# A language-model tower on one core: the first normalisation's statistics as running sums on ScalarE

## The reference

```python
h = weight[ids] * keep_mask[ids]                  # (32, 512, 256)
n = (h - mean(h)) / sqrt(var(h) + 1e-5)           # first normalisation, over the 256
u, res = split(n @ in_proj_w.T, [512])            # 512 and 256 wide
u = causal_conv(u, conv_w, taps=4) + conv_b       # along the tokens, channel by channel
g = u * sigmoid(softplus(u @ dt_proj_w.T + dt_proj_b))
y = scan(state = 0.9 * state + 0.1 * g)           # along the tokens
h = h + y @ out_proj_w.T + res                    # h2 in the kernel
n2 = (h - mean(h)) / sqrt(var(h) + 1e-5)          # second normalisation
h = h + quantised(n2) @ quantised(ffn_w).T + ffn_b
```

## Time and profile before

| | |
|---|---|
| median of 3 runs | 1020.15 us (1020.0 to 1021.33) |
| the profiled execution | 1021.15 us |
| its span, first to last instruction | 1019.3 us |
| PE busy | 956.8 us (94%) |
| DVE busy | 946.7 us (93%) |
| ACT busy | 577.6 us (57%) |
| POOL busy | 721.3 us (71%) |
| mean granted PE clock | 0.991 of full speed |

### The profile page before, as it was taken

How to read it: one execution, slowest core, us unless ns; L and a number is a source line. 1 busy time by engine, 2 the same in 40 slices (tenths; PEclk the granted TensorE clock), 3 DMA queues, 4 the chain that set the end, 5 groups by cost and what they waited for, 6 DMA issues and landing times.

```text
span 1019.3 us, 14858 instructions
## 1 busy us (share of the span) xinstructions
PE 956.8 (94%) x4892; PEld 788.0 (77%) x4892; DVE 946.7 (93%) x1594; ACT 577.6 (57%) x966; POOL 721.3 (71%) x586
## 2 busy tenths in 40 slices
PE   3599999999999999999999999999999999999996
PEld 2377888788788888878887878878887888787885
DVE  4779999999999999999999999999999999999866
ACT  4455655655565665565565556566556556555441
POOL 5656777877677877677788767787767777876561
PEclk9899999999999999999999999999999999999998
DMA  4223323334323434333334432343433343442201
GB/s 150 62 63 95 90 86 105 116 112 125 95 81 92 124 103 124 107 86 95 103 105 122 123 93 78 97 124 103 124 103 86 96 106 103 124 124 84 77 28 41
DMA packets 73787, 100.78 MB, mean 99 GB/s; under 512 B 12576, under 2 KB 61088, under 8 KB 73760
## 3 DMA queue, kind: packets, MB, share of 16 engines
q1 hardware_dynamic: 67616, 83.59, 26.7%
q0 software_dynamic: 6144, 16.85, 7.5%
HBM read 51.65 MB, written 48.76 MB: 99 GB/s over the span
## 4 chain that ended last, share of the span: by engine, by line
PE 48%; POOL 26%; issue 14%; DVE 8%; ACT 4%; DMA 1%; POOLq 0%; DVEq 0%
POOL g_lo L370 7%; PE psZ L1033 6%; POOL u_lo L377 6%; POOL rows L355 6%; PE psZ L1026 6%; PE psZ L1027 5%; POOL h L402 3%; PE psT L984 3%; PE psU L969 3%; PE psT L980 3%; PE psU L965 3%; PE psT L981 3%; PE psU L966 3%; ACT n L541 2%; PE psO L1070 2%
## 5 line engine op out<-in xcount | busy, mean ns | idle before, releaser
L370 POOL TENSOR_TENSOR g_lo<-g,g_hi 128x512 fp32r<-128x512 f32 x128 | 201.6, 1586 | 210.4 <-ACT g_hi L499 210.4
L707 DVE SCALAR_TENSOR_TENSOR u<-psU,cw,u 128x511 f32<-128x511 f32 x378 | 258.2, 739 | 4.2 <-ACT u L481 1.5
L1026 PE MATMUL psZ<-u_hi,dt_hi 128*128 128x512 f32 x512 | 204.0, 399 | 12.8 <-ACT u_hi L488 6.8
L1033 PE MATMUL psZ<-u_lo,dt_hi 128*128 128x512 f32 x512 | 206.6, 404 | 6.7 <-POOL u_lo L377 5.6
L1027 PE MATMUL psZ<-u_hi,dt_lo 128*128 128x512 f32 x512 | 203.2, 397 | 0.0
L377 POOL TENSOR_TENSOR u_lo<-u,u_hi 128x512 fp32r<-128x512 f32 x128 | 163.0, 1296 | 11.4 <-ACT u_hi L488 10.6
L499 ACT ACTIVATE g_hi<-g 128x512 fp32r<-128x512 f32 x128 | 77.0, 625 | 132.0 <-DVE g L791 131.9
L355 POOL DMA_INDIRECT rows<-table,ids x128 | 126.1, 985 | 30.9 <-issue 29.6
L488 ACT ACTIVATE u_hi<-u 128x512 fp32r<-128x512 f32 x128 | 80.5, 629 | 109.9 <-DVE u L707 106.0
L1033 PEld LDWEIGHTS psZ<-u_lo,dt_hi 128*128 128x128 f32 x512 | 96.6, 189 | 44.5 <-POOL u_lo L377 21.9
L1026 PEld LDWEIGHTS psZ<-u_hi,dt_hi 128*128 128x128 f32 x512 | 96.8, 189 | 32.3 <-issue 7.2
(11 more groups left out here) (110 smaller groups left out, 2181.7 us busy)
## 6 DMA issues: line engine op xcount, KB each, us to landing
turned_n<-nb_blocks SPq DMA_DIRECT2D x31, 512.0 KB
nT<-turned_n SPq DMA_DIRECT2D x124, 128.0 KB
out<-h SPq DMA_DIRECT2D x31, 512.0 KB, 2.9
turned<-xb SPq DMA_DIRECT2D x30, 512.0 KB, 2.6
xT<-turned SPq DMA_DIRECT2D x120, 128.0 KB
rows<-table,ids POOLq DMA_INDIRECT x128
dt_stage<-dt_wT SPq DMA_DIRECT2D x1, 1024.0 KB, 5.7
g<-in_wT SPq DMA_DIRECT2D x1, 768.0 KB, 4.7
```

Of the source, the lines that this page charges most:

```text
L370: pool.tensor_tensor(g_lo[:, m, :], g[:, m, :], f32(g_hi[:, m, :]), ALU.subtract).then_inc(g_lo_ready[m], 1)
L707: dve.scalar_tensor_tensor(u[:, m, back:T], u_psum_tile(st, m)[:, 0:T - back], cw[:, m, TAPS - 1 - back:TAPS - back], u[:, m, back:T], ALU ...
L1026: pe.matmul(psZ[:, m % 2, :], dt_hi[:, k, o], u_hi[:, k, :], start=(k == 0), stop=False)
L1033: ins = pe.matmul(psZ[:, m % 2, :], dt_hi[:, k, o], u_lo[:, k, :], start=False, stop=(k == M - 1))
```

## The change

The mean and the variance of the first normalisation no longer come from `bn_stats` and `bn_aggr`, apart from those of sequence 0. `mask_rows` gives out the sum of each masked row as it writes it (`accum_out`). GpSimd makes `-mean` and `-mean / 16` of it. ScalarE then takes the square of `(h - mean) / 16`, and the running sum of those 256 squares is the variance; GpSimd adds the epsilon. The squares themselves are written to `n1` and are not used.

The first normalisation is made for sequence `s + 2` at the end of `u`'s part of step `s`, instead of for `s + 1` at its beginning, and `turn_n1` and its transfers go with it. `split_nT` still works on sequence `s + 1`, whose transfers are then those of the step before; it stands one place earlier on VectorE and one place later on ScalarE. `nm2` and `ve2` of the second normalisation are made by GpSimd at the head of `inverse_root2`. The four gathers of a step fetch sequence `s + 3` and stand behind `inverse_root2`; `add_bias` goes to the head of GpSimd's step. Six small constant tiles are set at the start in place of two.

```diff
-        ids = sb("ids", [P, 2, C], I32)
+        ids = sb("ids", [P, RING, C], I32)
...
@@ SyncE @@
-                if st.front:
-                    sp.wait_ge(nT_lo_ready, s + 1)
-                    sp.wait_ge(n_turned, s + 1)
+                for ahead in st.turn_ahead:          # (1, 2) in step 0, then (2,)
+                    sp.wait_ge(n_turned, s + ahead)
+                    sp.wait_ge(nT_lo_ready, s + ahead)
...
@@ GpSimd @@
+                def mean1(ahead):
+                    pool.wait_ge(h_ready, s + ahead + 1)
+                    pool.tensor_tensor(nm1[:], sum1[:], minus_mean[:], ALU.mult)
+                    pool.tensor_tensor(nm1_part[:], sum1[:], minus_mean_part[:],
+                                       ALU.mult).then_inc(mean1_ready, 1)
+
+                def variance1(ahead):
+                    pool.wait_ge(square1_ready, s + ahead)
+                    pool.tensor_tensor(ve1[:], square1[:], eps[:], ALU.add).then_inc(var1_ready, 1)
...
                 def inverse_root2(part):
-                    pool.wait_ge(var2_ready, s + (part or 0))
+                    pool.wait_ge(aggr2_done, count)
...
+                    pool.tensor_tensor(nm2[:, cs], mv2[:, cs, 0], minus_1[:, cs], ALU.mult).then_inc(mean2_ready, 1)
+                    pool.tensor_tensor(ve2[:, cs], mv2[:, cs, 1], eps[:, cs], ALU.add).then_inc(var2_ready, 1)
...
-                if st.front:
-                    inverse_root1()
+                if st.tail:
+                    add_bias()
                 if st.back:
                     split_g(M - 1, s - 1)
-                if st.gather:
-                    gather(st.b, st.ring(2)[0], (0, 1))
-                if st.main:
-                    split_u(0)
-                    split_u(1)
-                if st.gather:
-                    gather(st.b, st.ring(2)[0], (2, 3))
-                if st.tail:
-                    add_bias()
+                if st.first:
+                    variance1(1)
+                    inverse_root1(1)
+                if st.early:
+                    mean1(2)
+                split_u(0)
+                split_u(1)
+                if st.early:
+                    variance1(2)
+                    inverse_root1(2)
...                                                # split_u(2), (3), split_xT
                 if st.back:
                     inverse_root2(None)
+                if st.gather:
+                    gather_ahead()                 # the four gathers of s + 3
...                                                # split_g(0) to (2)
@@ ScalarE @@
                         ins = act.activation(h[:, ring, c, :], h[:, ring, c, :], ACT.Copy,
-                                             scale=rows[:, ring, c, D:D + 1])
+                                             scale=rows[:, ring, c, D:D + 1], accum_out=sum1[:, c:c + 1])
...
+                def square1_rows(ahead):
+                    ring = st.ring(ahead)[0]
+                    act.wait_ge(mean1_ready, s + ahead)
+                    n1_free(ahead)
+                    for c in range(C):
+                        ins = act.activation(n1[:, c, :], h[:, ring, c, :], ACT.Square, bias=nm1_part[:, c:c + 1],
+                                             scale=ROOT_SCALE, accum_out=square1[:, c:c + 1])
+                    ins.then_inc(square1_ready, 1)
...
-                if st.front:
-                    normalise1()
+                    square1_rows(1)                # in step 0 alone
                 split_u(0)
                 split_u(1)
+                if st.first:
+                    normalise1(1)
+                if st.early:
+                    mask_rows(2)
+                    square1_rows(2)
                 if not st.first:
                     first_tap(2)
                     first_tap(3)
-                split_u(2)
                 if st.tail:
                     split_xT()
+                split_u(2)
                 split_u(3)
                 if st.early:
-                    mask_rows(2)
+                    normalise1(2)
+                tanh(0)
                 if st.front:
                     split_nT()
-                tanh(0)
                 tanh(1)
@@ VectorE @@
                     ins.then_inc(aggr2_done, 1)    # in variance2
-                    dve.wait_ge(aggr2_done, s + (part or 0))
-                    dve.tensor_scalar(nm2[:, span(part)], mv2[:, span(part), 0], -1.0, None, ALU.mult)
-                    dve.tensor_scalar(ve2[:, span(part)], mv2[:, span(part), 1], LN_EPS, None,
-                                      ALU.add).then_inc(var2_ready, 1)
...
                 convolve(0, 1, 0, 1, 0, 1)
-                if st.front:
-                    turn_n1()
+                if st.first:
+                    turn_n1(1)
...
                 if st.early:
-                    statistics1(2)
-                    variance1(2)
+                    turn_n1(2)
                 gate(0)
+                if st.front:
+                    split_nT()
                 gate(1)
...
-                if st.front:
-                    split_nT()
```

More of the change, by code:

```diff
@@ L227, in __init__ @@
                 self.early = not known or s + 2 < NSEQ
-                self.gather = not known or 0 <= s and s + 2 < NSEQ
-                self.load = not known or 0 <= s and s + 3 < NSEQ
+                self.gather = not known or s + 3 < NSEQ
+                self.load = not known or 0 <= s and s + 4 < NSEQ
                 self.first = known and s == 0
+                self.turn_ahead = (1, 2) if self.first else (2,) if self.early else ()
                 self.second = known and s == 1
@@ L862, in turn_blocks, with turn_n1 @@
                     dve.transpose(xb[:], flat(xd[:])).then_inc(xb_ready, 1)
[L864 to L868 removed]
+                def turn_n1(ahead):
+                    dve.wait_ge(n1_ready, s + ahead + 1)
+                    if not (st.first and ahead == 1):
+                        dve.wait_ge(n_written, 16 * (s + ahead - 1))
                     dve.transpose(nb_blocks[:], flat(n1[:])).then_inc(n_turned, 1)
```

123 lines of the change are left out of this document (66 added, 57 removed).

## The result

| | before | after |
|---|---|---|
| median, six executions each | 1021.47 us | 1025.73 us |
| the profiled execution | 1021.15 us | 1026.02 us |
| its span | 1019.3 us | 1024.2 us |
| DVE busy | 946.7 us (93%) | 829.8 us (81%) |
| ACT busy | 577.6 us | 647.2 us (63%) |

The kernel after is slower by 0.47%: ratio 1.0047, interval [1.0031, 1.0063]. 1023 us had been forecast. VectorE lost 117 us of work and the kernel lost 4.3.

What follows compares the result with a forecast made beforehand. PE's work and VectorE's load were taken as bounds, then a chain over ScalarE: 27 steps at 0.13 us more make 3.5, less 1.0, plus 0.2, on 1021.15: 1023.9, put at 1023 us; range 1010 to 1034.

Steps and rivals of the forecast that it cites:

- The chain of five terms: Steady step: tap sums, `linear`, `in_proj`, masks, squares form a loop through four engines, 29.51 us plus eight running sums.
- The price of a running sum: ScalarE's masks and squares: each sum costs one more 128x1 operand access, 0.092 us; eight per step make 0.74.
- the number named in advance: Sign of being right, on ScalarE: the four masks take 2.07 us; 1.7 us would show it wrong.
- the 31.1 us of that estimate: Rival, steady step: each read-out pays full price, 0.19 us, giving a 31.1 us step and 1045 us; chance 0.21.
- The ends: Lead-in and first steps gain 1.0 us, between 3 of gain and 1.5 of loss; the tail costs 0.2 us.
- GpSimd's `g_lo(3)` up to 0.6 us late: Output projection: `add_bias` now precedes `g_lo(3)`, up to 0.6 us late; the stall only eats into that ahead of `linear`.
- The mutual waits: VectorE and GpSimd: waits move from `nT_lo` to `dequantise` beside `g_lo`, up to 0.6 us; 0.05 us per step added.
- the fourth gather would wait for `quantise`: GpSimd's last gather: if held, `g_lo(0)` starts after `dequantise` and VectorE isn't held; if not, `dequantise` is held 0.6 us.
- two bounds: Kernel before, steady step of 30.17 us: VectorE busy 29.2 us, and PE losing 1.0 us to stalls.
- PE's own work: PE's work in a step costs 29.2 us at full granted clock, so steady steps can give at most 1.0 us each.

Runs made afterwards that it cites:

- Experiment 1: Kernel after without the eight running sums of masks and squares, so mean and variance are not computed: 1003.82 us, ratio 0.9827.
- Experiment 5: Kernel after, start reordered, squares behind `split_u(3)`, first normalisation's root and `normalise1` in the next step, `add_bias` behind `u_lo(1)`: 996.18 to 1047.77 us, median 1023.27.
- Experiment 2: Kernel after with `split_nT` ahead of `mask_rows(2)` in the lead-in and `linear_lo` ahead of `convolve(2, ...)` in step 1: 1019.51 us, ratio 0.9985.
- experiments 9 to 11: Kernel before: first without sequence s + 2's statistics, 0.9942; then with only the gathers moved behind `inverse_root2`, 1.0089; then with both edits, 1.0039.
- experiments 10 and 11: Kernel before with the four gathers, for s + 3, behind `inverse_root2`: 1029.52 us; the same also without sequence s + 2's statistics: 1025.63 us.

## Why the prediction was right, point by point

- **The chain of five terms** (steps 1 to 5). Right, and two experiments confirm it. In the steps around 520 us: tap sum to `linear` 8.80 (8.69 forecast), `linear` to `in_proj(0)` 8.31 and 8.51 (8.52), to the masks 7.70 to 7.79 (7.71), masks to squares 2.53 (2.54), squares to tap sum 2.78 (2.79). The step is 30.23 us; 30.30 was forecast. Experiment 1 took the read-outs away and gave 29.48, where the sum without them is 29.51. Experiment 5 took the squares out of the chain, and sixteen steps ran in 28.36 us.
- **The price of a running sum.** The size was right (0.09), the reason not. I had priced it as one more pointer operand; it is an instruction. The four masks take 2.07 us (519.72 to 521.79), the number named in advance. The 224 cycles of 1.2 GHz that "VectorE: DVE Perf Modes" of the Trainium skill has in its section on the TRN2 errata come to an estimate of 187 ns. A read-out is as long in the trace, 187 ns in the mean of 252; whether for that reason, no run shows. Half of it lies beside the activation, so the step did not get the 31.1 us of that estimate.
- **The ends: the term that was mis-sized.** -1.0 us was forecast, +4.5 measured by the start of step 3. It is made of four parts: step 0 starts 1.96 us later, for `split_nT` of the lead-in stands behind the masks with their read-outs; step 0 is 3.78 shorter; step 1 is 3.53 longer and step 2 is 2.79. I had looked at step 0 alone.

  Step 0 is shorter, but not for the forecast's reason. I had VectorE free of `dt_lo` and the first taps 3 us earlier. Another operation of VectorE, with its operands in SBUF, was held beside `dt_lo` in place of `nm`, for 5.09 us where the same took 0.68 before, and the first tap sum starts at 30.16 in place of 30.70:

```profile
24.01 5.09 DVE L728 SCALAR_TENSOR_TENSOR n<-h,n 128x512 f32<-128x512 f32 x1
```
```profile
L484 POOL TENSOR_TENSOR dt_lo<-dt_stage,dt_hi 128x2048 fp32r<-128x2048 f32 x1 | 5.1, 5113 | 2.4 <-ACT dt_hi L496 2.4
```

  `dt_proj(2)` of step 0 starts at 47.73 in place of 47.92. Before, TensorE had waited 3.76 us for a gate there, and did the rest of the step in 7.24 us at a granted clock of 0.76; after, it waits 0.09 and takes 5.61 at 1.00.

  In step 1 TensorE's merge needs `ffn_lo`, which stands behind `convolve(2, ...)`, and this one now waits for masks and squares:

```profile
66.86 4.29 DVE L757 SCALAR_TENSOR_TENSOR u<-psU,cw,u 128x511 f32<-128x511 f32 x6 [2.97 <-ACT u L515]
71.06 0.68 DVE L742 TENSOR_TENSOR ffn_lo<-psO,ffn_hi 128x512 fp32r<-128x512 f32 x1
```
```profile
71.79 1.11 PE L1051 MATMUL psO<-ident,scanned 128*128 128x128 f32 x4 [3.31 <-DVE ffn_lo L742]
```

  The wait was 1.60 us before, with the clock at 1.00 behind it. After a wait of 3.31 the granted clock is 0.61 for 7.2 us, a mean between its two levels of 1.2 and 2.4 GHz, which costs some 2.8 us more. Experiment 2 gave 3.25 us less than before at the start of step 3. In step 2 TensorE waits 0.32, 0.28 and 0.58 us for `g_lo`, and within 0.01 us the same in experiment 2; before, it waited for none of them.
- **How much of the agreement is luck.** The forecast had 3.5 us more in the steady steps and 0.8 less at the ends; measured are 1.7 more in the steady steps, 4.5 more ahead of step 3 and 1.3 less from step 30 on. The errors are -1.8, +5.5 and -1.5 us, and partly cancel. The mechanism and the steady step were forecast; that the total came within 3 us of the forecast is in part luck.
- **GpSimd's `g_lo(3)` up to 0.6 us late.** No such stall in 25 of the 27 steady steps: it ends at 519.31 and its matmul starts at 519.36. In step 2, and once more around 820 us, it comes to 0.57 and 0.58 us.
- **The mutual waits.** `dequantise` takes 1.60 in place of 1.22 us, 0.38 longer, and it is off the chain: right. That the fourth gather would wait for `quantise` as the one at the start did: not in the kernel after, since there the gather starts first (509.60 against 509.79); with `q` first it takes 1.80 us (experiment 5). The Trainium skill, "SBUF — State Buffer", "Who interferes with whom", infers no such effect; 0.95 against 1.80 us for a gather in one kernel speaks against that inference.
- **What holds the kernel before.** I named two bounds, VectorE's load and PE's stall on `xT_lo`. Neither alone nor both together give more than 0.6% when relieved (experiments 9 to 11). A third was not in the list: VectorE's operations that meet a row of GpSimd. That it is what keeps experiments 10 and 11 above 30 us is read from their traces and the sum of the loop; no run takes it away by itself, and the waits of TensorE for `g_lo` there (0.64 and 0.73 us a step) were not tested apart from it. This third bound was in the rows, as 1.67 us for `nm` and 2.16 for `nT_lo`, but I took it for a constant cost rather than one that follows GpSimd's row wherever it is moved.
- **PE's own work.** 29.2 us a step was too much, and so a steady step could give 1.8 us and not 1.0: steps 30 and 31 of the kernel after and sixteen of experiment 5 take 28.36 us, with 154 matmul records as in step 2 of before, at a granted clock of 1.00.

## What to carry to other kernels

Work taken from a full engine pays only where the chain that goes round once per iteration gets shorter; here it put masks, squares and eight read-outs on that chain, and the kernel with 117 us less of VectorE was 4 us slower. Write down the closed chain first, for the steady step and once more for each of the first iterations, where one-off operations stand behind the moved ones. And where VectorE and GpSimd both work on SBUF, look at the order in which they start: half a microsecond decided whether the same operation took 1.6 or 5.1 us.

## What the runs showed of the hardware

- ScalarE's running sum is read out by an instruction of its own: 0.19 us long, 0.09 us from start to start.
- `dequantise`, issued in the last 0.2 us of the last gather, was kept out until GpSimd's whole row had ended: 7.41 us with 6.2 us of row, 5.03 to 5.10 with 3.8, 2.60 where a wait broke the row after 1.3, 1.21 where another gather followed. `q` and `dequantise` together were kept out 79 times of 79 when issued 0.12 to 0.62 us before that gather's end, and 0 times of 92 at 0.64 to 0.76 us. Issued 1.2 us into the row, `dequantise` got in after one operation. `bscale` on 128x32, issued 0.2 to 0.3 us into a row of two, was kept out to its end (2.30 to 2.42 us in place of 0.18). Why it goes one way or the other is not settled by these runs.
- Beside one long operation of GpSimd (`dt_lo`, 4.6 and 5.1 us) whichever operation VectorE had there was held: `nm` for 4.56 us, a `scalar_tensor_tensor` on 128x512 for 5.09.
- A gather takes 0.95 us. Issued 0.25 us after the start of `q` it took 1.80, and 0.57 us after that of `dequantise` 1.47. In the fourteen traces no gather took over 1.2 us unless a VectorE operation with two operands in SBUF was running as it began.
- Behind a wait of 3.31 us TensorE's granted clock was 0.61 for 7.2 us, behind one of 2.87 us it was 0.50 for 3.42 us; behind one of 1.60 us it stayed at 1.00.
- TensorE's matmuls of 512 columns follow each other every 229 to 233 ns, at a granted clock of 1.00 in both cases. What sets the 2% between them stays open.
